# A mixture-of-experts stage: 31 whole token tiles become 17 whole tiles and 7 tiles of two halves, each half with its own expert's weights

## The reference

```
x = x + xattn(layernorm(x), ctx_768)     # 16 heads, 4096 keys per batch
x = x + attn(layernorm(x))               # 16 heads, a window of 64
x = x + ffn(layernorm(x))                # 16 experts, the best 2 for each token

logits = tensor @ Wr + br;  probs = softmax(logits)
topv, topi = top_k(probs, 2);  gate = sum(one_hot(topi) * topv)
h = relu(tensor @ W1[e] + b1[e])         # 256 -> 1024
y = h @ W2[e] + b2[e]                    # 1024 -> 256
out = sum over e of gate[e] * y[e]
```

## Time and profile before

| | us |
|---|---|
| median of 3 runs | 1372.64 |
| lowest, highest | 1368.77, 1376.05 |
| the profiled execution, its own time | 1374.4 |
| its span, first to last instruction | 1372.6 |
| mean granted TensorE clock | 0.963 of 2.4 GHz |

### The profile page before, as it was taken

The page is one execution under the profiler, slowest core; times in us unless marked ns, Lnnn a source line. Parts: engine busy times, 40 slices in busy tenths (PEclk is TensorE's granted clock), DMA queues, the critical chain, the costliest instruction groups (busy, mean ns, idle before and its releaser), DMA issues.

```text
span 1372.6 us, 29997 instructions
## 1 busy us (share of the span) xinstructions
PE 1275.8 (93%) x12347; PEld 764.3 (56%) x12347; DVE 883.9 (64%) x1706; ACT 710.0 (52%) x923; POOL 271.6 (20%) x262
## 2 busy tenths in 40 slices
PE   7779999999999999999999999999998539999996
PEld 4444444555444455544455544445665339999994
DVE  6788888676888776798867688825456452222224
ACT  4247777676777666677767577863332101111110
POOL 5141212111121121112111121020121112222220
PEclk9999999999999999999999999999998559999997
DMA  7553574533365344455533254100000059999953
GB/s 221 82 75 48 86 158 67 76 56 48 53 124 115 53 63 64 62 104 118 80 48 53 48 83 64 49 1 9 2 1 16 16 189 412 370 324 337 321 179 104
DMA packets 48360, 150.23 MB, mean 109 GB/s; under 512 B 17040, under 2 KB 21152, under 8 KB 40288
## 3 DMA queue, kind: packets, MB, share of 16 engines
q1 hardware_dynamic: 43664, 135.59, 43.1%
q0 software_dynamic: 2976, 8.13, 1.8%
q10 hardware_dynamic: 1584, 4.59, 0.9%
HBM read 88.63 MB, written 6.16 MB: 69 GB/s over the span
## 4 chain that ended last, share of the span: by engine, by line
PE 87%; DVE 5%; ACT 3%; issue 2%; DMA 1%; SPq 0%; POOL 0%; ACTq 0%; DVEq 0%; POOLq 0%
PE psum L545 20%; PE psum L527 14%; PE psum L505 10%; PE psum L882 8%; PE psum L894 8%; PE psum L426 7%; PE psum L443 6%; ACT wts L957 2%; PE psum L617 2%; DVE part_max L1171 1%; PE psum L721 1%; PE psum L611 1%; PE psum L651 1%; PE psum L689 1%; PE psum L573 1%
## 5 line engine op out<-in xcount | busy, mean ns | idle before, releaser
L1171 DVE TENSOR_REDUCE part_max<-psum 128x1 f32<-128x512 f32 x1024 | 656.1, 686 | 176.9 <-PE psum L505 175.4
L957 ACT ACTIVATE wts<-psum 128x1024 f32<-128x1024 f32 x512 | 516.1, 1023 | 93.8 <-PE psum L527 92.7
L545 PE MATMUL psum<-wts,vals 128*17 128x256 f32 x4096 | 317.3, 385 | 0.0
L527 PEld LDWEIGHTS psum<-queries,keys 51*128 51x128 f32 x2048 | 157.5, 185 | 200.1 <-issue 144.1
L527 PE MATMUL psum<-queries,keys 51*128 51x256 f32 x2048 | 259.8, 332 | 7.9 <-ACT wts L957 7.0
L505 PE MATMUL psum<-keys,queries 51*128 51x512 f32 x1024 | 228.9, 442 | 25.1 <-DVE part_max L1171 15.2
L1111 ACT ACTIVATE hid<-psum,b1s 128x128 f32<-128x128 f32 x124 | 35.4, 368 | 206.1 <-PE psum L882 206.1
L545 PEld LDWEIGHTS psum<-wts,vals 128*17 128x17 f32 x4096 | 69.5, 95 | 120.3 <-issue 97.0
L505 PEld LDWEIGHTS psum<-keys,queries 51*128 51x128 f32 x1024 | 97.4, 185 | 41.9 <-DVE part_max L1171 28.1
L882 PE MATMUL psum<-xTt,w1s 128*128 128x128 f32 x992 | 117.0, 277 | 0.2 <-DVE xTt L1494 0.2
L882 PEld LDWEIGHTS psum<-xTt,w1s 128*128 128x128 f32 x992 | 114.3, 193 | 0.6 <-issue 0.6
(11 more groups left out here) (201 smaller groups left out, 888.6 us busy)
## 6 DMA issues: line engine op xcount, KB each, us to landing
keys<-key_high SPq DMA_DIRECT2D x256, 128.0 KB, 4.4
w1s<-in_W SPq DMA_DIRECT2D x31, 1024.0 KB
w2s<-in_W SPq DMA_DIRECT2D x31, 1024.0 KB
keys<-key_low SPq DMA_DIRECT2D x128, 128.0 KB, 6.1
ctx_in<-in_ctxT SPq DMA_DIRECT2D x12, 768.0 KB, 8.7
ctx_in<-in_ctxT ACTq DMA_DIRECT2D x4, 768.0 KB, 10.5
queries<-query_high SPq DMA_DIRECT2D x64, 32.0 KB, 4.6
queries<-query_low SPq DMA_DIRECT2D x32, 32.0 KB, 4.8
```

Source lines behind the costliest of these rows:

```text
L527: m = e.matmul(bank(S_BANKS[S_NO["s", n] % 2] + i)[:, hh * SEQ:(hh + 1) * SEQ], keys[64 * i:64 * i + STK, hh, c, at:at + P], queries[g % 3 ...
L545: i = e.matmul(bank(O_BANK)[32 * j:32 * j + VW, 0:SEQ], vals[:, t, h * VW:(h + 1) * VW], wts[n % NW][:, j * SEQ:(j + 1) * SEQ], start=(t = ...
L957: i = e.activation(wts[n % NW], s_bank(job, 2), ACT.Exp, scale=QSCALE)
L1171: e.reduce_max(part_max[g % 2][:, hq, c:c + 1], bank(M_BANKS[n % 3]), AX_X).then_inc(dve_max, 1)
```

## The change

Tile numbers 0 to 16 stay whole. Tile numbers 17 to 23 are split: slots 0 to 63 belong to one expert, slots 64 to 127 to another (or to the same), and each half has a weight load of its own. The loads remain 31 in number (17 + 2 x 7). The tiles are worked off in the order whole, whole, split, seven times, and then three whole ones (`ORDER`); `LOADS` lists the weight loads in that order.

An expert with h pairs left over beyond its whole tiles takes a half where up to 64 are left, and a whole tile otherwise; the routing works this out with other comparisons, and the owners are computed one to a partition and moved into one row by a small float32 product on PE.

For a split tile `up` swaps the operands: 64 tokens are the stationary operand, 512 columns of W1 move, and the result has tokens on the partitions, 0 to 63 for one half and 64 to 127 for the other. Since `down` needs hidden features on the partitions, ACT and DVE copy the 2 x 512 raw values to `hid_raw`, PE turns them with 8 transposes (`turn_hidden`), and bias and relu follow on 64 columns at a time.

```diff
-SLOT_TILES = NSEL * TOK // P + BANKS - 1
+H = P // 2
+FULL, SPLIT = 17, 7
+TILES = FULL + SPLIT
+PLACES = 2 * TILES
+ORDER = [t for _s in range(SPLIT) for t in (2 * _s, 2 * _s + 1, FULL + _s)] + list(range(2 * SPLIT, FULL))
+LOADS = [(2 * _t + _h, _j) for _j, _t in enumerate(ORDER) for _h in range(1 if _t < FULL else 2)]
...
 # PE
+            e.wait_ge(dve_owns, 1)
+            e.matmul(bank(2)[0:1, 0:len(LOADS)], ownerf, identf[:, 0:len(LOADS)], start=True, stop=True).then_inc(pe_owner, 1)
...
             def up(j):
-                e.wait_ge(ld_w12[j % RING], 48 * (j // RING + 1))
+                w = weights(j)
                 e.wait_ge(dve_xT, j + 1)
                 for hb in range(2):
                     if j > 1:
                         e.wait_ge((act_h, dve_h)[hb], j - 1)
+                    dst = bank(2 * (j % 2) + hb)
+                    if split(j):
+                        for k in range(KE):
+                            for half in range(2):
+                                rows = slice(half * H, half * H + H)
+                                i = e.matmul(dst[rows], xTt[j % 2][:, k, rows], w1s[w[half]][:, k, hb * CH:(hb + 1) * CH],
+                                             start=(k == 0), stop=(k == KE - 1))
...
+            def turn_hidden(j):
+
+                for hb in range(2):
+                    e.wait_ge((act_raw, dve_raw)[hb], split_no(j) + 1)
                     for q in range(HC // 2):
+                        at = (hb * (HC // 2) + q) * P
+                        i = e.transpose(bank(2 * (j % 2) + hb)[:, q * P:(q + 1) * P], hid_raw[:, at:at + P], identf)
+                    i.then_inc(pe_hid, 1)
...
             def down(j):
...
+                    if split(j):
+                        for half in range(2):
+                            rows = slice(half * H, half * H + H)
+                            i = e.matmul(dst[rows], hid[j % 2][:, hc, rows], w2s[w[half]][:, hc],
+                                         start=(hc == 0), stop=(hc == HC - 1))
...
-            for s in range(SLOT_TILES + 2):
+            for s in range(TILES + 2):
...
+                if 1 <= s < TILES + 1 and split(s - 1):
+                    turn_hidden(s - 1)
...
 # ACT
+                if split(j):
+                    n = split_no(j)
+                    if n:
+                        e.wait_ge(pe_hid, 2 * n)
+                    e.activation(hid_raw[:, 0:CH], src, ACT.Copy).then_inc(act_raw, 1)
+                    e.wait_ge(pe_hid, 2 * n + 1)
...
 # DVE, expert loop
+            def raw(j):
+
+                e.wait_ge(pe_up, 2 * j + 2)
+                if split_no(j):
+                    e.wait_ge(pe_hid, 2 * split_no(j))
+                e.tensor_copy(hid_raw[:, CH:], bank(2 * (j % 2) + 1)).then_inc(dve_raw, 1)
...
-                if 1 <= s < SLOT_TILES + 1:
-                    hidden(s - 1)
+                if 1 <= s < TILES + 1:
+                    (raw if split(s - 1) else hidden)(s - 1)
                 if s >= 2:
                     result(s - 2)
+                if 1 <= s < TILES + 1 and split(s - 1):
+                    hidden(s - 1)
...
 # SP
-            def load_tile(j):
-                i = j % RING
-                if j >= RING:
-                    e.wait_ge(pe_y, j - RING + 1)
-                owns = e.value_load(owner[0:1, j:j + 1], min_val=0, max_val=BANKS - 1)
+            def load_weights(n):
+                i, j = n % RING, LOADS[n][1]
+                if n >= RING:
+                    e.wait_ge(pe_y, LOADS[n - RING][1] + 1)
+                owns = e.value_load(owner[0:1, n:n + 1], min_val=0, max_val=BANKS - 1)
```

More of the change, by code:

```diff
@@ L47, with load_of, split, split_no @@
 RING, XRING, YRING = 6, 5, 3
+PLACES = 2 * TILES
+ORDER = [t for _s in range(SPLIT) for t in (2 * _s, 2 * _s + 1, FULL + _s)] + list(range(2 * SPLIT, FULL))
+LOADS = [(2 * _t + _h, _j) for _j, _t in enumerate(ORDER) for _h in range(1 if _t < FULL else 2)]
+def load_of(j, half=0):
+    return LOADS.index((2 * ORDER[j] + half, j))
+def split(j):
+    return ORDER[j] >= FULL
+def split_no(j):
+    return sum(split(i) for i in range(j))
 STEPS = GROUPS * KT
@@ L299, in build @@
         gT = s4.tile("gT", (TOK,))
[L300 to L303, removed]
+        cmp = s4.tile("cmp", (2, BANKS, TT))
+        tiles = s4.tile("tiles", (2, 2 * BANKS))
+        ends = [s4.tile(f"ends{i}", (2, 2 * BANKS)) for i in range(2)]
+        start = s4.tile("start", (2, BANKS))
+        ends_row = s4.tile("ends_row", (BANKS,))
+        own_rows = s4.tile("own_rows", (BANKS,))
+        start_row = s4.tile("start_row", (BANKS,))
+        halves = s4.tile("halves", (BANKS,))
+        back = s4.tile("back", (BANKS,))
+        twice = s4.tile("twice", (BANKS,))
+        leap = s4.tile("leap", (BANKS,))
+        half_of = s4.tile("half_of", (BANKS,))
+        owns = [s4.tile(f"owns{i}", (BANKS,)) for i in range(3)]
+        ownerf = s4.tile("ownerf", (1,))
         slot_of = s4.tile("slot_of", (TT, BANKS))
+        past = s4.tile("past", (TT, BANKS))
         slotf = s4.tile("slotf", (2 * TT,))
[L306 to L311, removed]
+        owner = s4.tile("owner", (len(LOADS),), I32)
+        reached = s4.tile("reached", (2 * TT, TILES + 1))
+        at_tile = s4.tile("at_tile", (2 * TT, TILES))
+        in_tile = [s4.tile(f"in_tile{i}", (2 * TT, TILES), BF16) for i in range(2)]
         tiles_in = s4.tile("tiles_in", (2 * TT,))
@@ L871, in turn, with weights @@
                 i.then_inc(pe_x, 1)
+            def weights(j):
+                loads = [load_of(j, half) for half in range(2 if split(j) else 1)]
+                for n in loads:
+                    e.wait_ge(ld_w12[n % RING], 48 * (n // RING + 1))
+                return [n % RING for n in loads]
             def up(j):
-                e.wait_ge(ld_w12[j % RING], 48 * (j // RING + 1))
+                w = weights(j)
                 e.wait_ge(dve_xT, j + 1)
@@ L1110, in _ @@
                 for q in range(HC // 2):
-                    i = e.activation(hid[j % 2][:, q], bank(2 * (j % 2))[:, q * P:(q + 1) * P], ACT.Relu,
-                                     bias=b1s[j % RING][:, q:q + 1])
+                    for half in range(2 if split(j) else 1):
+                        cols = slice(half * H, half * H + H) if split(j) else slice(0, P)
+                        i = e.activation(hid[j % 2][:, q, cols], src[:, q * P:(q + 1) * P][:, cols], ACT.Relu,
+                                         bias=b1s[load_of(j, half) % RING][:, q:q + 1])
                 i.then_inc(act_h, 1)
@@ L1443, in _ @@
[L1443 to L1447 removed]
+            last_tile = src[:, :, BANKS:]
+            e.tensor_tensor(halves, own_tiles[:, 1], own_tiles[:, 0], ALU.subtract).then_inc(own.up(), 1)
@@ L1667, in _ @@
                 norm2(p)
+            for t in (tiles, ends[0], ends[1]):
+                e.memset(t[:, :, 0:BANKS], 0.0).then_inc(pool_ends0, 1)
             def load_rows(j):
@@ L1686, in _ @@
             e.wait_ge(dve_to, 1)
[L1687 to L1688 removed]
+            for s in range(TILES + 2):
+                if s + 3 < TILES:
                     load_rows(s + 3)
@@ L1825, in layouts @@
     p = np.arange(P)
+    place = np.concatenate([[w for w, _ in LOADS], np.full(P - len(LOADS), PLACES)])
     bqkv = i["L0_attn_b_qkv"]
```

173 lines of the change are left out of this document (103 added, 70 removed).

## The result

| | before | changed |
|---|---|---|
| median of 4 runs, us | 1371.63 | 1335.34 |
| lowest, highest | 1368.77, 1376.05 | 1329.88, 1337.78 |
| span of the profiled run | 1372.6 | 1328.1 |
| ratio of the runs | | 0.9727 (95% interval 0.9687 to 0.9768) |

The change makes the kernel 2.7% faster, 36.3 us by the medians. The forecast was 1332 us, 3.0% faster.

What follows compares the result with a forecast made beforehand. PE was taken to bound the kernel, DMA close behind. The profiled 1374.4 us less 40.7 for the loop plus 0.3 for routing gave 1334.0, as a median 1332; own range 1326 to 1338, with rivals up to 1352.

Steps and rivals of the forecast that it cites:

- The bound before and the price of a whole tile: Expert loop: PE is the bound, a whole tile takes 7.24 us, DMA has a margin of 1.27.
- Halves side by side: Split tile: both 64-column halves run beside each other on PE, `up` 3.43 us and `down` 3.46.
- Switches, 0.70 a split tile: Split tile: entering and leaving the divided array twice costs PE 0.70 us, bounds 0 and 1.0.
- Transposes, 0.86: Split tile: the eight transposes of `turn_hidden` take 0.86 us on PE, raw copies hidden beside `down`.
- Loop: Expert loop: 17 whole tiles at 7.24 us and 7 split at 8.66 give 183.7, 40.7 us less.
- Routing, +0.3: Routing ahead of the loop: 0.3 us longer, bounds 0 to +1.5, with `owner` 0.7 us later.
- DMA: Weight loads: at 413 GB/s the last lands 10 us before its use; DMA decides from 388 GB/s downwards.
- rival 1: DMA becomes the loop's bound, PE waiting ahead of `up`: 1341 us at 370 GB/s, 1362 at 331; chance 15%.
- Buffers: Six weight buffers suffice: some 15 us from a buffer's release to its use, and a load takes 5.7.
- Rival 2: Split tiles: one half's weights aren't loaded under the other's product, 2.45 us each, 17 in all, 1349 us; chance 5%.

Runs made afterwards that it cites:

- halves_apart: Changed kernel with each split tile's products ordered all of one half, then all of the other; loop 205.3 us against 186.4, kernel 1356.0 us.
- more_weights: Changed kernel with 0.524 MB more for each weight load; loop 215.2 us against 186.4, kernel 1366.6 us.
- split_free: Changed kernel with split tiles computed in whole form, first half's weights alone, leaving out the second halves' experts; loop 180.1 us against 186.4, kernel 1333.9 us.
- late_split: Changed kernel with the first split tile fourth, not third; loop 185.5 us against 186.4, kernel 1336.4 us.
- five_buffers: Changed kernel with 5 weight buffers in place of 6; loop 212.7 us against 186.4, kernel 1367.5 us.
- splits_last: Changed kernel with the 17 whole tiles first and the 7 split ones last; loop 201.8 us against 186.4, kernel 1356.6 us.

## Why the prediction was right

- **The bound before and the price of a whole tile.** 7.24 us in all kernels. Right.
- **Halves side by side.** 3.43 and 3.46 forecast; 3.58 and 3.60 measured, with the 0.15 of entering the divided array in each. Right. It hangs on the order of the products, as halves_apart shows; the change had the right order, but the prediction did not say that it mattered.
- **Switches, 0.70 a split tile.** Read off the chain: 0.15 into `up`, 0.19 behind it, 0.14 into `down`, 0.15 behind it, 0.63 in sum. Right; the lower bound of 0 is ruled out.
- **Transposes, 0.86.** 0.87, with no wait for a raw copy.
- **Loop.** Forecast 40.7 us less, measured 39.1. The rest: a wait of 1.1 at the first split tile, which the prediction had seen as just possible and had left out, and a clock that rose later in the first `up` (5.68 us against 4.86; it took 5.0 to 6.0 in the experiments, and why it rose later than before is open). Split and whole tiles alone give 17 x 7.24 + 7 x 8.64 = 183.6, 40.8 less.
- **Routing, +0.3.** From `cmp` to the first `up` 20.12 us, 19.45 before, so +0.7, of which 0.24 up to `at_row` and 0.5 in the row load's landing. `owner`, done 4.36 us after the start of `cmp` and 3.59 before, came 0.8 later, forecast 0.7:

```profile
1100.77 0.42 DVE L1504 TENSOR_TENSOR cmp<-psum,tile_size 128x256 f32<-128x256 f32 x1 [0.29 <-PE psum L890]
...
1104.96 0.17 DVE L1554 CAST owner<-psum 1x31 int32<-1x31 f32 x1
```

- **DMA.** Close behind, as forecast: the last load's packets ended 167.5 us into the loop, some 8 us ahead of its use, for which 10 were forecast (402 GB/s from 1135 to 1280, in place of 413). That it is the second bound is shown by more_weights and split_free. The prediction names a fall of the clock among the signs of being wrong, but rival 1's sum has no such term and is too low: in more_weights the clock cost 10.1 us beside 18.7 of waits.
- **Buffers.** The 5.7 us for a load were wrong, and here the prediction had luck. With five buffers, where the queue runs dry in between, the second weight load of a split tile lands 9.3 to 10.2 us after its issue (from the second split tile on), and only 7.6 lie between release and use. With six there are 15.9, as forecast, but the queue is full and the load takes longer. In the changed kernel the second load of the second split tile is issued at 1143.19, its last weight packet ends at 1155.13, and the last of its landing events comes at 1157.47, 0.8 us ahead of the `up`. In late_split the same loads land 12.7 to 14.1 us after their issue, 1.0 to 2.3 us ahead of their use. So six buffers suffice by 1 to 2 us, and not by the 10 that 15 less 5.7 leave.

```profile
1143.19 0.34 SPq L1900 DMA_DIRECT2D w1s<-in_W  x1
```

- **Rival 2** (weights not loaded under the other half's product): 8.64 us leave no room for another 2.45. Refuted.

The spans differ by 44.5 us, more than loop and routing explain. The other 6.2 us lie ahead of the routing, in stages that the change leaves alone: the changed kernel's profiled run was the fastest of its four, and in its first 60 us the granted clock was 1.00, against 0.89 before. The medians, 36.3 apart, agree with 39.1 - 0.7 within the interval of the ratio.

## What to carry to other kernels

When two products with half the columns each are to share the array, write them alternately: in float32 here, a reach of about four records was all that made up for another order. Before fewer tiles are bought with more bytes per us, work out the rate at which DMA takes over. Then count the time of a load from issue to landing, with its neighbours in the queue, against the path from the buffer's release to its use. A short wait of PE, here up to 2.1 us, cost its own length; longer ones mostly cost the clock as well.

## What was not expected of the hardware

- PE started records of the other half while three of the first half's still waited, and 3.8 records overlapped at each border, in blocks of four and of eight. The Trainium skill, TensorE: Matmul & The Clock Gate, Part 3 (The mechanism), has products start in strict program order; the two runs disagree by those 3.8 records.
- Changing between the whole and the halved array cost 0.14 to 0.19 us each way in float32, with no wait in the queue.
- DMA held 413 GB/s for 165 us with a backlog, but in the mean only 339 GB/s from 1150 to 1300 with five buffers, when its queue ran dry between loads.
- Behind ten of the eleven waits of 2.5 to 4.2 us in more_weights, five_buffers and splits_last (and one of 6.0) the next split `up` took 5.0 to 6.5 us in place of 3.65, with the granted clock at its lower level, 1.2 GHz, for part or all of it; behind those of up to 2.1 us, and one of 2.7, it took 3.65.
